# ScalarE in place of GpSimd multiplies the inputs of sequences 8 to 11 by their 1/rms in a diffusion block with attention

## Chip, cores and metric

One core of a Trainium2 chip runs the whole program in one launch. The metric is the device time of one execution in microseconds (us). The engines have separate instruction streams that run in program order and meet only at semaphores: TensorE (PE), VectorE (DVE), ScalarE (ACT), GpSimd (POOL) and SyncE (SP, which only issues transfers here).

## Reference

The input has 16 sequences of 128 tokens with 128 channels, all in float32. A transformer block with modulation by a condition (its first half is attention) is followed by a block of linear attention. What matters for the change is the beginning of the first block:

```python
def rmsnorm(x, w, eps=EPS):
    v = jnp.mean(x * x, axis=-1, keepdims=True)
    return w * (x * jax.lax.rsqrt(v + eps))

h = modulate(rmsnorm(x, norm1_w), sh_msa, sc_msa)   # x * (1 + scale) + shift, per sequence
qkv = (h @ qkv_w.T).reshape(B, N, 3, H, D)          # 16 heads of 8
q, k = rmsnorm(q), rmsnorm(k); q, k = rotated by the positions
attn = softmax(q @ k.T * D ** -0.5)
x = x + g_msa * ((attn @ v) @ proj_w.T + proj_b)
```

After that come a gated feed-forward network, and a second block with softmax over queries and keys, a context matrix per head, a layer norm and an output projection.

## The kernel before

One sequence (128 tokens on the partitions, 128 channels) is the unit of the attention part. After a prologue that brings sequences 0 to 5 through the projections, a loop of steps t = 0, 1, ... runs on four engines at once. It is written out by hand for each engine, and each engine works on another sequence of the pipeline in the same step. In step t, for the places that the change touches:

- **Input, sequence t+8.** `input_normed(b)` writes `xs` = x times `rstd_x`, a column with 1/rms of every token. `xs` has four buffers (NXS = 4). Sequences 0 to 3 are done by VectorE, 4 to 7 by ScalarE in the prologue, 8 to 15 by GpSimd in its steps 0 to 7 (L1114 to L1127).
- **1/rms of sequences 8 to 15.** GpSimd makes the column for all eight at once in its step 0, at the head of `input_normed(8)`: an affine operation on the mean squares (L1120) and a power of -1/2 (L1122), which raises the semaphore `p_rstd` to 3. The mean squares come from ScalarE before its step 0.
- **Projections, sequence t+6.** TensorE transposes `xs` (`input_turned(t + 6)`, L1962), ScalarE scales the result into `hT`, TensorE multiplies by the weights (L1969), and ScalarE copies q and k to `qk` and writes their squares to `sq`.
- **Heads, sequences t+5 and t+4.** VectorE sums the squares (`square_sums(t + 6)`, L1672) and for every odd sequence makes a first guess of 1/sqrt for two sequences at once (`seeds`, L1682 to L1687). GpSimd rotates q and k (`turned_partner(t + 5)`, `turned_own(t + 5)`, `added(t + 4)`), refines the guess in ten small operations in its even steps (`rsqrt_of_heads(t + 5)`, L1157 to L1175), and multiplies (`normed(t + 4)`, L1197, tile `qkpad`).
- **Keys and queries, sequence t+3.** TensorE transposes `qkpad` (`queries_and_keys(t + 3)`, L1940) once `normed` of that sequence is done; VectorE spreads the result over `kBD` (L1637) and `qTs` (L1645).
- **Scores, sequence t+2, and exponents, sequence t.** `round_(t, r)` on TensorE, r = 0 and 1, interleaves the scores of t+2 (L1890), whose row maxima VectorE takes (`rowmax`, L1608), with the scores again for the exponents of t (L1899), to which ScalarE applies Exp (`exp`, L1307, tile `probs`, four banks a step). Round r waits until both Exp of the round before have read their banks (`s_p`), and until VectorE has the maxima of the round before (`s_max`).
- **Values, sequence t.** TensorE multiplies `probs` by the values (L1995); ScalarE copies the result at the end of its step (`summed(t)`, L1376), spreads the values of t+6 (`values`, L1360) and sums squares of a finished sequence (`spread_of(t - 2)`, L1316).

So the order of work in a step is, on GpSimd: `turned_partner`, `rsqrt_of_heads`, `added`, `normed`, `input_normed`, `turned_own`, `input_biased`; on ScalarE: two Exp, `queries_and_max`, `modulated_input`, two Exp, `attended`, `squares`, `queries_keys`, `summed`, `values`, `spread_of`. The rest of the program (feed-forward in the last steps and behind the loop, then the second block) follows the loop on the same queues. The functions that the change touches, and the loops that call them:

Of the kernel before, what the change touches and what calls it, by code (L numbers as in the profile page):

```python
# [65 lines left out]
HEAD_B, MID_B, EARLY = 4, 8, 2  # L66
FIFTH6, FIVE4, THREE2 = -5.0 / 3.0, 1.25, 1.5
FRONT_B = 6
TBL = 4 * DH

LAST_A, LAST_POOL = B + 2, B + 1
# [5 lines left out]
def is_seq(b):  # L77

    return not isinstance(b, int) or 0 <= b < B


def wait(eng, sem, value):

    if not isinstance(value, int) or value > 0:
        eng.wait_ge(sem, value)
# [27 lines left out]
def dit_then_linear_attention(nc, x, cond, pos, norm1_w, qkv_w, q_norm_w, k_norm_w, proj_w, proj_b,  # L113
# [3 lines left out]
    with ctx:  # L117
        def sb(name, shape, dt=F32):
            return ctx.enter_context(nc.sbuf_tensor(name, shape, dt))

        def sem(name):
            return ctx.enter_context(nc.semaphore(name))
# [57 lines left out]
        turns = sb("turns", [128, B * AXES])  # L180
        rope = sb("rope", [128, B, TBL])

# [107 lines left out]
        p_rstd = sem("p_rstd")  # L290
# [12 lines left out]
        s_xs = sem("s_xs")  # L303
# [142 lines left out]
        def front_bank(b):  # L446

            return bank[O_BANK if b < FRONT_B and b % 2 else W_BANK]

# [606 lines left out]
        def _(g):  # L1056
# [57 lines left out]
            def input_normed(b):  # L1114

                if not is_seq(b):
                    return
                if b == MID_B:
                    g.wait_ge(pv_a, A_SQUARES)
                    q.tensor_scalar(ms[:, MID_B:], ms[:, MID_B:], 1.0, EPS0, ALU.mult, ALU.add).then_inc(p_ms, 1)  # L1120
                    g.wait_ge(p_ms, 1)
                    q.tensor_tensor(rstd_x[:, MID_B:], ms[:, MID_B:], minus_half[:, 0:B - MID_B], ALU.pow).then_inc(p_rstd, 1)  # L1122
                    g.wait_ge(p_rstd, 3)
                    g.wait_ge(s_xs, MID_B)
                wait(g, s_xsT, b - NXS + 1)
                q.tensor_tensor(xs[b % NXS][:, :], xin[:, b, :], rstd_x[:, b:b + 1].to_broadcast([128, D]),
                                ALU.mult).then_inc(s_xs, 1)  # L1127
# [128 lines left out]
        def _(a):  # L1256
# [44 lines left out]
            def exp(t, r, i):  # L1301

                if not is_seq(t):
                    return
                a.wait_ge((s_e0, s_e1)[i], ROUNDS * t + r + 1)
                wait(a, s_o, ROUNDS * (t - 1) + r + 1)
                q.activation(probs[2 * r + i][:, :, :, :].rearrange("p f a t -> p (f a t)"), exp_bank(t, r, i)[:, :],  # L1307
                             ACT.Exp, scale=SCALE).then_inc(s_p, 1)

            def spread_of(b):  # L1310

                if not is_seq(b):
                    return
                a.wait_ge(s_x1, b + 1)
                wait(a, s_sq1, b)
                q.activation(squared[:, :], x1[:, b, :], ACT.Square, scale=D ** -0.5, accum_out=ms1[:, b:b + 1]).then_inc(s_sq1, 1)  # L1316

            def modulated_input(b):

                if not is_seq(b):  # L1320
                    return
                a.wait_ge(s_xsT, b + 1)
                wait(a, s_qkv, b - 1)
                q.activation(hT[b % 2][:, :], front_bank(b)[:, 0:T], ACT.Identity, bias=mod(b, S1), scale=mod(b, A1)).then_inc(s_hT, 1)  # L1324

            def queries_and_max(b):

                if not is_seq(b):
                    return
                a.wait_ge(s_tp, b + 1)  # L1330
                wait(a, s_e0, ROUNDS * (b - 1))
                wait(a, s_e1, ROUNDS * (b - 1))
                q.activation(qTm[b % 2][:, :, :].rearrange("p f t -> p (f t)"), bank[P_BANK][:, 0:2 * T], ACT.Copy).then_inc(s_qTm, 1)

            def squares(b):

                if not is_seq(b):
                    return
                a.wait_ge(s_qkv, b + 1)
                wait(a, s_ss, b - 1)  # L1340
                q.activation(sq[b % 2][:, :, :].rearrange("p h d -> p (h d)"), front_bank(b)[:, 128:128 + 2 * D], ACT.Square).then_inc(s_sq, 1)

            def queries_keys(b):

                if not is_seq(b):
                    return
                wait(a, s_pa, b - NQK + 1)
                wait(a, s_r1, b - NQK + 1)
                q.activation(qk[b % NQK][:, :, :].rearrange("p h d -> p (h d)"), front_bank(b)[:, 128:128 + 2 * D], ACT.Copy).then_inc(s_qk, 1)  # L1349

            def values(b):

                if not is_seq(b):
                    return
                wait(a, s_o, ROUNDS * (b - NVP + 1))
                if b < NVP:
                    a.wait_ge(seeded_g, 2 * b + 2)
                spread = vpad[b % NVP][:, :].rearrange("p (a c) -> p a c", a=2)[:, :, 0:8 * VSTEP].rearrange(
                    "p a (i c) -> p i a c", c=VSTEP)[:, :, :, 0:DH]
                q.activation(spread, front_bank(b)[:, 384:512].rearrange("p (i a d) -> p i a d", i=8, a=2), ACT.Copy).then_inc(s_v, 1)  # L1360

            def attended(b):

                if not is_seq(b):
                    return
                a.wait_ge(s_oTp, b + 1)
                wait(a, s_proj, b)
                q.activation(oT[:, :], bank[P_BANK][:, 256:384], ACT.Copy).then_inc(s_oT, 1)

            def summed(b):  # L1370

                if not is_seq(b):
                    return
                a.wait_ge(s_o, ROUNDS * (b + 1))
                wait(a, s_oq, b)
                q.activation(oT4[:, :], bank[O_BANK][:, 0:2 * T], ACT.Copy).then_inc(s_oT4, 1)  # L1376
# [12 lines left out]

            def input_normed(b):  # L1390

                a.wait_ge(p_rstd, 2)
                a.wait_ge(s_xs, b)
                a.wait_ge(s_xsT, b - NXS + 1)
                q.activation(xs[b % NXS][:, :], xin[:, b, :], ACT.Identity, scale=rstd_x[:, b:b + 1]).then_inc(s_xs, 1)
# [29 lines left out]
            queries_keys(3)  # L1425
            values(3)
            input_normed(4)
            input_normed(5)
            modulated_input(4)
            weights(P_W1, bank[P_BANK][:, 0:FC * 128], w1T[:, :], 1.0)  # L1430
# [21 lines left out]
            for t in range(LAST_A):  # L1452
                exp(t, 0, 1)
                exp(t, 0, 0)
                if t == B - 1:
                    b_first(t - B)
                if t >= B:
                    b_first(t - B)
                if t >= B - 2:
                    b_input(t - B, t % 2)  # L1460
                queries_and_max(t + 1)
                modulated_input(t + 6)
                exp(t, 1, 0)
                exp(t, 1, 1)
                if t < B:
                    attended(t - 1)
                squares(t + 6)
                queries_keys(t + 6)
                if t >= B - 1:
                    b_rest(t - B)  # L1470
                if t >= B:
                    attended(t - 1)
                summed(t)
                values(t + 6)
                spread_of(t - 2)
                if t == B - 6:
                    a.wait_ge(ld_rest, N_REST)
                    q.activation(outw[:, :], outw_n[:, :], ACT.Copy, scale=0.5).then_inc(pv_a, 1)
                    q.activation(nbb[:, :], ident[:, :], ACT.Identity, bias=par[:, R_NB:R_NB + 1], scale=0.0).then_inc(pv_a, 1)
                    q.activation(lin[:, :, :].rearrange("p c f -> p (c f)"), lin_n[:, :, :].rearrange("p c f -> p (c f)"), ACT.Identity,  # L1480
                                 scale=par[:, R_NG:R_NG + 1]).then_inc(pv_a, 1)
# [293 lines left out]
        def _(e):  # L1775
# [53 lines left out]
            def modulation_rows():  # L1829

                e.wait_ge(pv_a, A_GB)
                e.wait_ge(s_v, FRONT_B)
                for k, src in enumerate((modr[:, 2, :], gbias[:, :], modr[:, 5, :])):
# [122 lines left out]
            def input_turned(b):  # L1956
# [3 lines left out]
                e.wait_ge(s_xs, b + 1)  # L1960
                wait(e, s_v, b - 1 if b < FRONT_B else b)
                q.transpose(front_bank(b)[:, 0:T], xs[b % NXS][:, :], ident[:, :]).then_inc(s_xsT, 1)  # L1962
# [16 lines left out]
            def weighted_values(b, r):  # L1979
# [4 lines left out]
                if r == 0:  # L1984
                    e.wait_ge(s_v, max(b + 1, FRONT_B))
                    wait(e, s_on, b)
# [118 lines left out]
```

## Time and profile before

| | |
|---|---|
| median of 3 runs | 206.25 us (206.19 to 206.61) |
| the profiled execution | 207.28 us, of which the span from its first to its last instruction is 205.6 us |
| mean granted TensorE clock | 0.992 of full speed |
| PE busy | 180.2 us (88% of the span) |
| DVE busy | 164.2 us (80%) |
| POOL busy | 141.0 us (69%) |
| ACT busy | 129.8 us (63%) |

Times in the trace count from the first instruction of the span. A share of busy time is a mean over stages with different limits, so the stage around steps 0 to 5 (about 29 to 65 us) has to be read by itself, from the timeline of each engine. In a timeline each row has the start, the length, the engine, the line and the operation; what stands in brackets at the end is how long the engine was idle before it and who ended that.

### The profile page before, as it was taken

The page shows a single profiled execution, that of the slowest core. Times are in us where ns is not written, and L with a number is a line of the kernel's source. Part 1 is how long each engine was busy: PE and PEld are TensorE (multiplying, and loading weights), DVE is VectorE, ACT ScalarE, POOL GpSimd, SP SyncE. Part 2 cuts the span into 40 slices and gives each one's busy share as a digit, 9 for nine tenths or more (in the row PEclk, how much of TensorE's full clock was granted, in tenths as well). Part 3 has the DMA queues.
Part 4 walks back from the last instruction along what each step waited for, and adds up shares of the span by engine and source line. Part 5 has one row for each costly group of instructions (what it writes and reads, how often), then busy time and mean ns, then how long its engine had stood idle before and what let it go on. Part 6 is the DMA issues. An engine that isn't in the chain of part 4 may idle for free.

```text
span 205.6 us, 6098 instructions
## 1 busy us (share of the span) xinstructions
PE 180.2 (88%) x2039; PEld 141.5 (69%) x2039; DVE 164.2 (80%) x495; ACT 129.8 (63%) x379; POOL 141.0 (69%) x333
## 2 busy tenths in 40 slices
PE   2598887997999999999999778899998899999954
PEld 2355565786687777787766557799997578887742
DVE  6799899896989999898765235678888789999871
ACT  1367798675867777767664764444443468999630
POOL 8889798998989897979700890445534847586651
PEclk9999999999999999999999999999999999999997
DMA  5955006800000000000000000000000000011111
GB/s 94 281 144 207 0 10 271 341 6 0 3 3 2 5 5 0 3 3 2 3 3 3 2 0 3 0 2 0 5 0 2 0 3 0 0 32 51 51 37 42
DMA packets 10428, 8.32 MB, mean 40 GB/s; under 512 B 3105, under 2 KB 9886, under 8 KB 9886
## 3 DMA queue, kind: packets, MB, share of 16 engines
q1 hardware_dynamic: 7006, 7.25, 10.2%
q10 hardware_dynamic: 3392, 0.68, 1.6%
q8 instruction: 17, 0.28, 0.5%
q14 instruction: 13, 0.11, 0.2%
HBM read 6.86 MB, written 1.07 MB: 39 GB/s over the span
## 4 chain that ended last, share of the span: by engine, by line
PE 45%; DVE 14%; issue 8%; ACT 6%; POOL 3%; POOLq 0%; ACTq 0%; DVEq 0%
PE bank L1890 5%; PE bank L880 5%; PE bank L868 5%; PE bank L869 4%; PE bank L1995 4%; DVE qkpad L1608 4%; PE bank L1899 4%; PE bank L997 2%; ACT probs L1307 2%; PE bank L913 2%; PE bank L1940 2%; PE bank L1927 2%; PE bank L1969 2%; PE bank L1915 1%; PE bank L977 1%
## 5 line engine op out<-in xcount | busy, mean ns | idle before, releaser
L1608 DVE TENSOR_REDUCE qkpad<-bank 128x4 f32<-128x512 f32 x64 | 41.0, 684 | 10.4 <-PE bank L1890 9.4
L1307 ACT ACTIVATE probs<-bank 128x512 f32<-128x512 f32 x64 | 34.7, 594 | 20.6 <-PE bank L1899 19.8
L1890 PE MATMUL bank<-kBD,qTs 32*128 32x256 f32 x224 | 32.0, 399 | 3.3 <-DVE qkpad L1608 2.2
L1899 PE MATMUL bank<-qTm,kBD 32*128 32x128 f32 x448 | 32.5, 283 | 0.0
L1899 PEld LDWEIGHTS bank<-qTm,kBD 32*128 32x128 f32 x448 | 27.1, 186 | 0.0
L1890 PEld LDWEIGHTS bank<-kBD,qTs 32*128 32x128 f32 x224 | 19.9, 184 | 9.4 <-DVE qkpad L1608 4.9
L579 ACT ACTIVATE th<-bank 128x256 f32<-128x256 f32 x24 | 9.2, 384 | 20.4 <-PE bank L869 17.0
L1995 PE MATMUL bank<-probs,vpad 128*32 128x128 f32 x512 | 18.5, 277 | 2.9 <-ACT probs L1307 2.9
L1995 PEld LDWEIGHTS bank<-probs,vpad 128*32 128x32 f32 x512 | 12.6, 109 | 9.3 <-ACT probs L1307 8.5
L1969 PE MATMUL bank<-qkvT,hT 128*128 128x384 f32 x32 | 15.4, 578 | 0.5 <-ACT hT L1324 0.5
L678 DVE SCALAR_TENSOR_TENSOR yg<-th,bank 128x256 f32<-128x256 f32 x24 | 10.1, 419 | 6.5 <-ACT th L579 6.5
L1940 PE MATMUL bank<-ident,qkpad 128*128 128x128 f32 x96 | 14.1, 277 | 1.1 <-POOL qkpad L1197 1.1
L1135 POOL TENSOR_TENSOR partner<-qk,rope 128x96 f32<-128x96 f32 x32 | 14.2, 466 | 0.8 <-ACT qk L1349 0.8
L509 POOL TENSOR_TENSOR x<-fg,x 128x256 f32<-128x256 f32 x6 | 4.4, 728 | 15.0 <-DVE fg L695 15.0
L868 PE MATMUL bank<-hT,w1T 128*128 128x256 f32 x48 | 14.4, 382 | 0.0
L869 PE MATMUL bank<-hT,w3T 128*128 128x256 f32 x48 | 14.3, 379 | 0.0
L880 PE MATMUL bank<-w2T,ff 128*128 128x128 f32 x96 | 13.2, 275 | 0.0
L519 POOL TENSOR_TENSOR rstd<-var,minus_half 128x2 f32<-128x2 f32 (+1 forms) x17 | 11.7, 691 | 1.4
L1940 PEld LDWEIGHTS bank<-ident,qkpad 128*128 128x128 f32 x96 | 10.8, 141 | 2.8 <-POOL qkpad L1197 1.7
L880 PEld LDWEIGHTS bank<-w2T,ff 128*128 128x128 f32 x96 | 12.4, 191 | 0.4
L1146 POOL TENSOR_TENSOR rot<-qk,rope 128x256 f32<-128x256 f32 x16 | 11.6, 728 | 0.0
L1197 POOL TENSOR_TENSOR qkpad<-rot,ny 128x256 f32<-128x256 f32 x15 | 9.7, 647 | 2.2 <-DVE ny L1705 0.4
(254 smaller groups left out, 527.6 us busy)
## 6 DMA issues: line engine op xcount, KB each, us to landing
gate<-in_cond_dram SPq DMA_DIRECT2D x1, 1024.0 KB, 4.7
x<-gate_rows SPq DMA_DIRECT2D x1, 1024.0 KB, 4.2
y<-gate_rows SPq DMA_DIRECT2D x1, 1024.0 KB, 6.3
res<-gate_rows SPq DMA_DIRECT2D x1, 1024.0 KB, 9.7
out_dram<-res SPq DMA_DIRECT2D x7, 128.0 KB, 1.8
xin<-in_x_dram ACTq DMA_DIRECT2D x2, 256.0 KB, 5.4
xin<-in_x_dram SPq DMA_DIRECT2D x1, 512.0 KB, 5.6
ada_n<-in_L_cond_ada_w_dram SPq DMA_DIRECT2D x1, 256.0 KB, 6.2
```

Of the source, the lines that this page charges most:

```text
L519: q.tensor_tensor(rstd[:, rows], var[:, rows], minus_half[:, 0:rows.stop - rows.start], ALU.pow).then_inc(made, 1)
L868: q.matmul(bank[GU_BANK[c]][:, 0:UNIT * T], w1T[:, c * 128:c * 128 + 128], flat(hT2[1 - p]), start=True, stop=True)
L869: q.matmul(bank[GU_BANK[c]][:, UNIT * T:], w3T[:, c * 128:c * 128 + 128], flat(hT2[1 - p]), start=True, stop=True).then_inc(b_gu, 1)
L880: last = q.matmul(bank[F_BANK[j]][:, 0:D], ff[c][:, j * T:(j + 1) * T], w2T[:, c, :], start=c == 0, stop=c == FC - 1)
L1135: last = q.tensor_tensor(heads(partner[b % 2][:, :, :])[:, :, :, k::2], heads(qk[b % NQK][:, :, :])[:, :, :, 1 - k:ROPE:2], table(b, 1)[:, ...
L1307: q.activation(probs[2 * r + i][:, :, :, :].rearrange("p f a t -> p (f a t)"), exp_bank(t, r, i)[:, :], ACT.Exp, scale=SCALE).then_inc(s_p, 1)
L1608: q.tensor_reduce(out_, score_bank(b, r, i)[:, :].rearrange("p (f a t) -> p f a t", f=2, a=2), X_AXIS, ALU.max, negate=True).then_inc(s_ma ...
L1890: last = q.matmul(bank[S_BANK[i]][:, f * 2 * T:(f + 1) * 2 * T], qTs[b % 2][rows, f, :], kBD[b % NKB][rows, f, :, :].rearrange("p a t -> p ...
L1899: last = q.matmul(bank[E_BANK[i]][:, (2 * f + k) * T:(2 * f + k + 1) * T], kBD[t % NKB][rows, f, k, :], qTm[t % 2][rows, f, :], start=True ...
L1940: last = q.transpose(dst[:, at_ + f * T:at_ + (f + 1) * T], qkpad[b % NKB][:, s, 8 * f:8 * f + 8, :].rearrange("p h d -> p (h d)"), ident[ ...
L1969: q.matmul(front_bank(b)[:, 128:512], hT[b % 2][:, :], qkvT[:, :], start=True, stop=True).then_inc(s_qkv, 1)
L1995: last = q.matmul(bank[O_BANK][32 * c:32 * c + 32, r * T:(r + 1) * T], vpad[b % NVP][:, col:col + VSTEP], probs[2 * r + i][:, f, k, :], st ...
```

## The change

ScalarE gets `input_normed(t + 8)` as the last piece of its steps 0 to 3. GpSimd still makes the column of 1/rms at the same place of its step 0, then returns, and resumes the multiplications with sequence 12 in its step 4.

```diff
+BY_ACT = 12
...
@@ GpSimd, input_normed(b)
                     q.tensor_tensor(rstd_x[:, MID_B:], ms[:, MID_B:], minus_half[:, 0:B - MID_B], ALU.pow).then_inc(p_rstd, 1)
+                if b < BY_ACT:
+                    return
+                if b == BY_ACT:
                     g.wait_ge(p_rstd, 3)
-                    g.wait_ge(s_xs, MID_B)
+                    g.wait_ge(s_xs, BY_ACT)
                 wait(g, s_xsT, b - NXS + 1)
@@ ScalarE, input_normed(b)
-                a.wait_ge(p_rstd, 2)
+                a.wait_ge(p_rstd, 2 if b < MID_B else 3)
                 a.wait_ge(s_xs, b)
                 a.wait_ge(s_xsT, b - NXS + 1)
                 q.activation(xs[b % NXS][:, :], xin[:, b, :], ACT.Identity, scale=rstd_x[:, b:b + 1]).then_inc(s_xs, 1)
@@ ScalarE, end of step t
                 spread_of(t - 2)
+                if MID_B <= t + 8 < BY_ACT:
+                    input_normed(t + 8)
```

The order on ScalarE at the end of its step 0, before the change (`qk2` and `vpad6` are of sequence 6, `oT4` closes sequence 0, `probs1` and `probs0` are the first two Exp of step 1):

```order
L1349 ACTIVATE qk2<-bank7 128x256 [waits s_r1,s_pa]
L1376 ACTIVATE oT4<-bank6 128x256 [waits s_o]
L1360 ACTIVATE vpad6<-bank7 128x8x2x8 [waits seeded_g]
L1307 ACTIVATE probs1<-bank3 128x512 [waits s_o,s_e1]
L1307 ACTIVATE probs0<-bank2 128x512 [waits s_o,s_e0]
L1333 ACTIVATE qTm0<-bank5 128x256 [waits s_e1,s_e0,s_tp]
```

and with it:

```order
L1353 ACTIVATE qk2<-bank7 128x256 [waits s_r1,s_pa]
L1380 ACTIVATE oT4<-bank6 128x256 [waits s_o]
L1364 ACTIVATE vpad6<-bank7 128x8x2x8 [waits seeded_g]
L1399 ACTIVATE xs0<-xin,rstd_x 128x128 [waits s_xsT,s_xs,p_rstd]
L1311 ACTIVATE probs1<-bank3 128x512 [waits s_o,s_e1]
L1311 ACTIVATE probs0<-bank2 128x512 [waits s_o,s_e0]
```

A multiplication (`xs0`, sequence 8) that waits for `p_rstd` now stands between the last copy of step 0 and the first Exp of step 1; the same stands at the ends of steps 1, 2 and 3.

The order on GpSimd at the end of its step 0, before (`qkpad0` is `normed(4)`, `rot1` is `turned_own(5)`, `partner0` belongs to sequence 6):

```order
L1197 TENSOR_TENSOR qkpad0<-rot0,ny0 128x32x8 [waits s_tp,s_ad,s_newton]
L1120 TENSOR_SCALAR ms<-ms 128x8 [waits pv_a]
L1122 TENSOR_TENSOR rstd_x<-ms,minus_half 128x8 [waits p_ms]
L1126 TENSOR_TENSOR xs0<-xin,rstd_x 128x128 [waits s_xsT,s_xs,p_rstd]
L1146 TENSOR_TENSOR rot1<-qk1,rope 128x256 [waits s_qk]
L1135 TENSOR_TENSOR partner0<-qk2,rope 128x96 [waits s_qk]
L1135 TENSOR_TENSOR partner0<-qk2,rope 128x96
```

and with the change:

```order
L1201 TENSOR_TENSOR qkpad0<-rot0,ny0 128x32x8 [waits s_tp,s_ad,s_newton]
L1121 TENSOR_SCALAR ms<-ms 128x8 [waits pv_a]
L1123 TENSOR_TENSOR rstd_x<-ms,minus_half 128x8 [waits p_ms]
L1150 TENSOR_TENSOR rot1<-qk1,rope 128x256 [waits s_qk]
L1139 TENSOR_TENSOR partner0<-qk2,rope 128x96 [waits s_qk]
L1139 TENSOR_TENSOR partner0<-qk2,rope 128x96
L1186 TENSOR_TENSOR rot1<-rot1,partner1 128x32x6 [waits s_r1]
```

The column `rstd_x` stays where it was, and `turned_own(5)` now follows it at once, without the multiplication in between. The order on TensorE, VectorE and SyncE is the same in both kernels.

## Rows read from the trace of the kernel before

**Rows 1.** The chain that ended last: start, length, work.

```profile
48.99 0.64 POOL qkpad L1197
49.67 0.66 PE bank L1940 x4
```

**Rows 2.** Timeline of POOL, steps 0 and 2.

```profile
37.20 1.66 POOL L1122 TENSOR_TENSOR rstd_x<-ms,minus_half 128x8 f32<-128x8 f32 x1
38.93 0.40 POOL L1126 TENSOR_TENSOR xs<-xin,rstd_x 128x128 f32<-128x128 f32 x1
39.29 0.73 POOL L1146 TENSOR_TENSOR rot<-qk,rope 128x256 f32<-128x256 f32 x1
...
44.45 0.29 POOL L1157 TENSOR_TENSOR nt<-ny 128x64 f32<-128x64 f32 x1
...
48.99 0.63 POOL L1197 TENSOR_TENSOR qkpad<-rot,ny 128x256 f32<-128x256 f32 x1
```

**Rows 3.** Timeline of ACT, end of the prologue to step 4.

```profile
27.04 0.87 ACT L1395 ACTIVATE xs<-xin,rstd_x 128x128 f32<-128x128 f32 x2
...
35.71 0.27 ACT L1360 ACTIVATE vpad<-bank 128x128 f32<-128x128 f32 x1
36.62 1.09 ACT L1307 ACTIVATE probs<-bank 128x512 f32<-128x512 f32 x2 [0.63 <-PE bank L1899]
...
47.87 1.08 ACT L1307 ACTIVATE probs<-bank 128x512 f32<-128x512 f32 x2 [0.35 <-PE bank L1899]
```

**Rows 4.** Timeline of PE, steps 1 to 4.

```profile
37.37 0.27 PE L1962 MATMUL bank<-ident,xs 128*128 128x128 f32 x1
37.85 0.48 PE L1890 MATMUL bank<-kBD,qTs 32*128 32x256 f32 x2 [0.20 <-DVE qkpad L1608]
...
42.56 0.82 PE L1940 MATMUL bank<-ident,qkpad 128*128 128x128 f32 x6
...
43.48 0.48 PE L1890 MATMUL bank<-kBD,qTs 32*128 32x256 f32 x2
...
48.19 0.38 PE L1940 MATMUL bank<-ident,qkpad 128*128 128x128 f32 x2
...
50.37 0.48 PE L1890 MATMUL bank<-kBD,qTs 32*128 32x256 f32 x2
...
56.45 0.48 PE L1890 MATMUL bank<-kBD,qTs 32*128 32x256 f32 x2 [0.44 <-DVE qkpad L1608]
```

**Rows 5.** Timeline of DVE, steps 1, 4 and 6.

```profile
41.73 0.50 DVE L1687 TENSOR_SCALAR ny<-nms 128x64 int32<-128x64 int32 x1
...
53.29 0.41 DVE L1672 TENSOR_REDUCE nms<-sq 128x32 f32<-128x256 f32 x1
...
55.12 1.28 DVE L1608 TENSOR_REDUCE qkpad<-bank 128x4 f32<-128x512 f32 x2
...
65.34 0.41 DVE L1672 TENSOR_REDUCE nms<-sq 128x32 f32<-128x256 f32 x1
...
66.77 1.28 DVE L1608 TENSOR_REDUCE qkpad<-bank 128x4 f32<-128x512 f32 x2
```

**Rows 6.** Two stretches: length, PE busy (instructions), granted clock, DMA share, GB/s.

```profile
48.57:49.67 1.10, 0.00 (x1) 1.00 0.00 0
199.00:204.00 5.00, 3.27 (x15) 0.66 0.13 39
```

**Rows 7.** Timeline of PE near the end.

```profile
196.65 0.33 PE L913 MATMUL bank<-ident,xs 128*128 128x128 f32 x1 [0.90 <-DVE xs L821]
196.82 0.60 PE L850 MATMUL bank<-warm 128*128 128x256 bf16 x4
197.26 0.41 PE L950 MATMUL bank<-outw,hs 128*128 128x128 f32 x2
...
199.46 0.39 PE L913 MATMUL bank<-ident,xs 128*128 128x128 f32 x1 [1.18 <-DVE xs L821]
199.65 1.06 PE L850 MATMUL bank<-warm 128*128 128x256 bf16 x4
200.51 0.63 PE L950 MATMUL bank<-outw,hs 128*128 128x128 f32 x2
```

## Prediction

> **What bounds the kernel now.** I read the chain that ended last first, then the timelines of GpSimd, ScalarE, TensorE and VectorE over steps 0 to 6, then the granted clock. The chain begins on GpSimd: `normed(6)` ends at 48.99 + 0.64 = 49.63 us, and TensorE takes up its transposes 0.04 us later [rows 1]. From there the chain runs without a break through TensorE and VectorE to the end. So GpSimd is late exactly once: in step 3 TensorE has done two of its six transposes at 48.19 and must wait with the other four. How much that costs is seen by the distance from the transposes to the second round of scores: 43.48 - 42.56 = 0.92 us in step 2, 50.37 - 48.19 = 2.18 us in step 3, a difference of **1.26 us** [rows 4]. In all other places of steps 1 to 6 TensorE waits little (0.20 and 0.44 us, both for row maxima of VectorE [rows 4]). The reader should see that ScalarE is not in this chain at that place, but that TensorE's second round waits for two Exp of ScalarE in every step.
>
> **What the change takes away.** Four multiplications of GpSimd, in its steps 0 to 3. One of them moves the next instruction by 39.29 - 38.93 = 0.36 us [rows 2]. Two of the four lie ahead of `normed(6)`, so GpSimd alone could be 0.72 us earlier there; that is the whole gain, and it would come out of the 1.26 us. The other two lie behind it, where GpSimd has ceased to be late, and I cost them at nothing.
>
> **What it adds, step 0.** The column of 1/rms is made by GpSimd from 37.20 to 37.20 + 1.66 = 38.86 [rows 2], at the end of a queue that the change does not shorten: nothing is removed ahead of it. ScalarE has finished its step 0 at 35.71 + 0.27 = 35.98 and starts the Exp pair of step 1 at 36.62 [rows 3]. With the change the multiplication of sequence 8 stands between these two and needs the column. It can begin at 38.86 + 0.07 = 38.93 (0.07 is the handover that GpSimd's own multiplication shows [rows 2]), and takes 0.43, half of a pair of the same instruction in the prologue, 0.87 [rows 3]. So the Exp pair starts at 39.36 instead of 36.62, **2.74 us late**. Queued behind it on ScalarE are the Exp pair, `qTm`, `hT` of sequence 7, the second Exp pair, and the squares and copies of sequence 7. No table has to be loaded for it: the same function runs between the Exp already, as `hT`.
>
> TensorE has nothing to hide that. Its last transpose of step 1 ends at 37.37 + 0.27 = 37.64, and the second round started at 37.85 [rows 4]. Now it needs the Exp pair, which ends at 39.36 + 1.09 = 40.45; with a handover of 0.04 that is 40.49, **2.64 us later** than before, and TensorE stands still from 37.64 to 40.49, for 2.85 us. VectorE, which waits for the scores of that round, moves with it.
>
> **Steps 1 to 3.** Their multiplications have their column. They cost ScalarE 0.43 each, in gaps such as the 0.35 us ahead of the Exp pair at 47.87 [rows 3]. The excess of 0.08 stays hidden: that pair ends at 47.87 + 1.08 = 48.95, and TensorE would want it at 50.37 - 1.26 = 49.11 at the earliest [rows 3, 4]. Without this cover it would be 0.08 us a step.
>
> **What comes back in step 3.** The delay of 2.64 us makes TensorE reach the transposes at 48.19 + 2.64 = 50.83 [rows 4]. GpSimd is not free to use its lead: its refinement for sequence 7 waits for VectorE's guess, which ended at 41.73 + 0.50 = 42.23 [rows 5] and now ends at 44.87. With the handover it starts at 44.94 instead of 44.45 [rows 2], 0.49 late, and `normed(6)` ends at 49.62 + 0.49 = 50.11 [rows 2]. That is still ahead of TensorE, so the whole 1.26 us vanishes, though by TensorE's lateness and not by GpSimd's lead. Left: 2.64 - 1.26 = 1.38.
>
> **What comes back in step 4.** There the second round waited 0.44 us for VectorE [rows 4]. The same VectorE work, from the sum of squares to the maxima, took 55.12 - 53.29 = 1.83 us in step 4 and 66.77 - 65.34 = 1.43 us in step 6 [rows 5]. With GpSimd now waiting for VectorE, as it does in step 6, step 4 should look like step 6; I take 0.3 of these 0.40 us, between nothing and the whole 0.44. The delay is then **1.1 us** (0.94 to 1.38). Behind step 4 every engine is shifted alike, the chain is unbroken, and no transfer with a fixed time is left to meet, so I let it go through to the end.
>
> **The clock of TensorE.** A gap of 2.85 us between matmuls occurs nowhere in this part of the trace. At a gap of 1.10 us the granted clock stayed at full speed, 2.4 GHz [rows 6]. Near the end it fell: TensorE was idle for 0.90 us, worked, and was idle for 1.18 us [rows 7]; in the 5 us from 199 the mean clock was 0.66, which is (1 - 0.66) x 5 / 0.5 = 3.4 us at half speed, 1.2 GHz [rows 6]. The idle time before that fall, 2.08 us in two pieces, is less than the 2.85 us that the change makes in one. So I expect a fall here too, of about that length. Its price comes from the warm-up matmuls at either level: four of them advance in 197.26 - 196.82 = 0.44 us at full speed and in 200.51 - 199.65 = 0.86 us at half [rows 7]. A fully busy TensorE then loses 1 - 0.44/0.86 = 0.49 of the stretch, 1.66 us of 3.4; some 0.7 us of it should fall into the gap itself, which leaves 2.7 x 0.49 = **1.3 us**. Bounds: nothing (no fall), and 1.66.
>
> A rule speaks against this term. The Trainium skill (TensorE: Matmul & The Clock Gate, section Why this matters for your kernels) advises only to keep gaps between bursts of matmuls under a limit, and a single gap of this size would pass it; by that advice the sum would end without the clock term, as in the first rival. The fall behind the two shorter gaps [rows 7] does not agree with reading the advice as a guarantee.
>
> **Sum.** 1.1 + 1.3 = 2.4 us. The working was done inside one execution of 207.28 us (span 205.6), 1.03 above the median of the runs; as it consists of differences only, I add it to the median: 206.25 + 2.4 = 208.65, given as **208.6 us**.
>
> **Rivals.**
> 1. *The wait is paid, the clock holds.* 206.25 + 1.1 = 207.35 us, between 207.2 and 207.6. For it: the full clock through the gap of 1.10 us [rows 6]; against it: the fall near the end. Chance 0.27.
> 2. *The clock is low for two such stretches,* because the first is followed by a TensorE that still waits for VectorE. 208.65 + 1.3 = 209.95 us. For it: TensorE was still meeting waits of 0.44 us in step 4 [rows 4]; against it: at half speed TensorE is the slow engine and hardly idle. Chance 0.07.
> 3. *Faster: ScalarE does not wait in step 0, and GpSimd's lead counts.* The place is the column of 1/rms: if it were written before 36.62 - 0.43 - 0.07 = 36.12, the multiplication would vanish in ScalarE's gap, and `normed(6)` would come 0.72 us earlier: 206.25 - 0.72 = 205.53 us. It is written at 38.86 [rows 2], 2.7 us past that point; only GpSimd's spans in the profile being far too long would save it. Chance 0.04.
> 4. *The delay is made up on the way,* because work behind step 4 has slack that the chain does not show: 206.25 us or a little more. The unbroken chain speaks against it. Chance 0.04.
>
> That the change does not do what it says is excluded by the order: ScalarE's stream has the four instructions more and GpSimd's four fewer.
>
> **How the numbers follow.** The forecast has 0.58; its own range is 206.25 + 0.94 + 1.0 = 208.2 to 206.25 + 1.38 + 1.66 = 209.3. With the first rival, 0.85 of the chance lies between 207.2 and 209.3, which I widen by 0.1 each way for the spread of the runs: 207.1 to 209.4. A measurement of this kernel tells about 0.2% (0.4 us) from no change. Faster by more than that is rival 3, 0.04; within it is rival 4, 0.04; slower are the forecast and rivals 1 and 2, 0.92.
>
> **What would show it.** Right: ScalarE idle for nearly 3 us ahead of the multiplication of sequence 8, released by the line that makes the column; TensorE idle for about 2.85 us ahead of the second round of step 1; no wait for `qkpad` in step 3; GpSimd waiting for VectorE's guess already at sequence 7. The clock term is right if the granted clock shows some 3.4 us at half speed at about 39 to 46 us. Wrong: an Exp pair of step 1 that starts before 38 us; a TensorE that still waits for `normed(6)`; or a distance to the old kernel that shrinks behind step 5, which would mean slack that I did not see.

## The result, and the profile after

The changed kernel takes **208.62 us** (median of 4 runs, 208.28 to 209.56) against 206.38 us (206.19 to 206.61): a ratio of 1.0113, with a 95% interval of 1.0087 to 1.0138. It is slower by about 1.1%, as forecast; the forecast time was 208.6 us, in a range of 207.1 to 209.4. The ratios in this document are of each kernel's fast executions and are no quotients of the two medians, from which they differ by up to 0.3%.

The profiled execution took 208.37 us with a span of 206.6. One thing has to be known before the two profiles are compared. In the one before, TensorE's clock was low for 3.4 us near the end [rows 6]; in the one after it was not, as the stretch from 199 to 206 us shows (columns as in rows 6):

```profile
199.00:206.00 7.00, 3.39 (x28) 1.00 0.19 56
```

The two spans differ by 1.0 us, but the kernels differ by more. The place to compare them is the loop, ahead of that stretch. The start of the second round of scores in each step, from the timelines of TensorE (us):

| step | 1 | 2 | 3 | 4 | 6 | 8 |
|---|---|---|---|---|---|---|
| before | 37.85 | 43.48 | 50.37 | 56.45 | 68.11 | 79.46 |
| after | 40.42 | 47.66 | 53.28 | 58.90 | 70.18 | 81.53 |
| later by | 2.57 | 4.18 | 2.91 | 2.45 | 2.07 | 2.07 |

The change loses 2.57 us in step 1, another 1.61 by step 2, and gets back 1.27 in step 3, 0.46 in step 4 and 0.38 by step 6. What stays is **2.07 us**, and it stays to the end: the same operation of VectorE starts at 198.58 us before (`xs`, L821) and at 200.65 after. The two lowest times of the kernel before are 206.19 and 206.25 us; 206.2 + 2.07 = 208.3 is about the two lowest of the change, 208.28 and 208.37.

**Step 0 and 1.** The timeline of ScalarE answers to [rows 3]:

```profile
35.74 0.27 ACT L1364 ACTIVATE vpad<-bank 128x128 f32<-128x128 f32 x1
38.91 0.40 ACT L1399 ACTIVATE xs<-xin,rstd_x 128x128 f32<-128x128 f32 x1 [2.90 <-POOL rstd_x L1123]
39.22 1.06 ACT L1311 ACTIVATE probs<-bank 128x512 f32<-128x512 f32 x2
...
51.60 0.40 ACT L1399 ACTIVATE xs<-xin,rstd_x 128x128 f32<-128x128 f32 x1
52.05 1.09 ACT L1311 ACTIVATE probs<-bank 128x512 f32<-128x512 f32 x2
```

ScalarE stands still for 2.90 us behind its last copy, released by the line that makes the column, and the Exp pair starts at 39.22 instead of 36.62. At the end of step 2 the same multiplication (51.60) needs no wait. The chain that ended last now runs through that column, some 12 us ahead of the `normed(6)` of [rows 1]:

```profile
37.22 1.67 POOL rstd_x L1123
...
39.69 0.60 ACT probs L1311
40.42 0.45 PE bank L1896
```

TensorE, to be set against [rows 4]:

```profile
37.40 0.27 PE L1968 MATMUL bank<-ident,xs 128*128 128x128 f32 x1
40.42 0.65 PE L1896 MATMUL bank<-kBD,qTs 32*128 32x256 f32 x2 [2.75 <-ACT probs L1311]
...
45.11 0.48 PE L1896 MATMUL bank<-kBD,qTs 32*128 32x256 f32 x2
...
47.66 0.48 PE L1896 MATMUL bank<-kBD,qTs 32*128 32x256 f32 x2
...
52.38 0.82 PE L1946 MATMUL bank<-ident,qkpad 128*128 128x128 f32 x6
...
53.28 0.48 PE L1896 MATMUL bank<-kBD,qTs 32*128 32x256 f32 x2
...
58.90 0.48 PE L1896 MATMUL bank<-kBD,qTs 32*128 32x256 f32 x2
```

The gap ahead of the second round of step 1 is 2.75 us, released by ScalarE's Exp. In step 3 all six transposes go in one piece (52.38), with no wait for `qkpad`; in step 4 there is no wait for row maxima (58.90). The granted clock in the stretches around the gap (columns as in rows 6):

```profile
37.40:40.42 3.02, 0.27 (x3) 1.00 0.96 399
40.42:40.70 0.28, 0.28 (x6) 0.85 0.08 29
40.70:44.00 3.30, 3.30 (x27) 0.50 0.02 7
44.00:45.00 1.00, 1.00 (x33) 0.99 0.00 0
```

It is at full speed, 2.4 GHz, through the gap, and falls to half, 1.2 GHz, just behind it, for about 3.4 us. In that time the first matmuls of the round take 0.65 us where they took 0.48, and TensorE arrives at step 2 another 1.61 us late.

**GpSimd**, to be set against [rows 2]:

```profile
37.22 1.65 POOL L1123 TENSOR_TENSOR rstd_x<-ms,minus_half 128x8 f32<-128x8 f32 x1
38.84 0.73 POOL L1150 TENSOR_TENSOR rot<-qk,rope 128x256 f32<-128x256 f32 x1
...
45.11 0.89 POOL L1139 TENSOR_TENSOR partner<-qk,rope 128x96 f32<-128x96 f32 x2 [2.32 <-ACT qk L1353]
46.36 0.29 POOL L1161 TENSOR_TENSOR nt<-ny 128x64 f32<-128x64 f32 x1 [0.36 <-DVE ny L1693]
...
50.76 0.63 POOL L1201 TENSOR_TENSOR qkpad<-rot,ny 128x256 f32<-128x256 f32 x1
...
55.28 0.46 POOL L1233 TENSOR_TENSOR xin<-xin,y 128x128 f32<-128x128 f32 x1
56.42 0.89 POOL L1139 TENSOR_TENSOR partner<-qk,rope 128x96 f32<-128x96 f32 x2 [0.68 <-ACT qk L1353]
```

`turned_own(5)` follows the column at 38.84, 0.45 us earlier than before. But the lead is lost: GpSimd waits 2.32 us for `qk` of sequence 7 from the late ScalarE, then for VectorE's guess, and `normed(6)` starts at 50.76 instead of 48.99.

### The profile page after: what moved, and what is told of

Read it like the earlier page. It is cut to its first block, busy times and chain, and to the rows that moved or that the text cites. A ratio compares the mean times of both kernels' runs of the same rounds, so it can differ in the third digit from the quotient of the medians.

```text
span 206.6 us, 6102 instructions
## 1 busy us (share of the span) xinstructions
PE 179.5 (87%) x2039; PEld 141.1 (68%) x2039; DVE 163.5 (79%) x495; ACT 131.0 (63%) x383; POOL 139.3 (67%) x329
## 4 chain that ended last, share of the span: by engine, by line
PE 56%; DVE 9%; issue 7%; ACT 6%; POOL 4%; POOLq 0%; ACTq 0%; DVEq 0%
PE bank L1896 8%; PE bank L2001 6%; PE bank L1905 5%; PE bank L881 5%; PE bank L869 5%; PE bank L870 4%; PE bank L1975 4%; PE bank L1946 3%; PE bank L1933 3%; ACT probs L1311 2%; PE bank L998 2%; PE bank L914 2%; DVE qkpad L1614 2%; PE bank L1941 1%; PE bank L1921 1%
## 5 line engine op out<-in xcount | busy, mean ns | idle before, releaser
L1896 PE MATMUL bank<-kBD,qTs 32*128 32x256 f32 x224 | 32.8, 406 | 5.0 <-ACT probs L1311 2.8
L1905 PE MATMUL bank<-qTm,kBD 32*128 32x128 f32 x448 | 33.3, 288 | 0.0
L1896 PEld LDWEIGHTS bank<-kBD,qTs 32*128 32x128 f32 x224 | 20.6, 187 | 11.0 <-issue 6.1
L1905 PEld LDWEIGHTS bank<-qTm,kBD 32*128 32x128 f32 x448 | 27.8, 190 | 0.0
L1975 PE MATMUL bank<-qkvT,hT 128*128 128x384 f32 x32 | 16.0, 596 | 0.5 <-ACT hT L1328 0.5
```

What stands on the lines that cost most here:

```text
L1896: last = q.matmul(bank[S_BANK[i]][:, f * 2 * T:(f + 1) * 2 * T], qTs[b % 2][rows, f, :], kBD[b % NKB][rows, f, :, :].rearrange("p a t -> p ...
L1905: last = q.matmul(bank[E_BANK[i]][:, (2 * f + k) * T:(2 * f + k + 1) * T], kBD[t % NKB][rows, f, k, :], qTm[t % 2][rows, f, :], start=True ...
L1975: q.matmul(front_bank(b)[:, 128:512], hT[b % 2][:, :], qkvT[:, :], start=True, stop=True).then_inc(s_qkv, 1)
```

## Experiments

The theory: ScalarE's wait for the column makes TensorE late (2.6 us, mostly made up by step 6) and makes its clock fall (1.6 us, not made up). The rivals: ScalarE's added work is the loss; or the low clock costs nothing; or the loss is in proportion to the wait. The first four kernels ran on one chip, beside a kernel before of 206.18 us (21 runs); the next four on another, beside 206.31 us (14 runs); four further profiles on a third, beside 205.97 us (one run).

**GpSimd keeps sequence 8.** ScalarE's multiplications stay at the ends of steps 1 to 3 only.

```diff
@@ GpSimd, input_normed(b)
-                if b < BY_ACT:
+                if MID_B < b < BY_ACT:
                     return
-                if b == BY_ACT:
+                if b in (MID_B, BY_ACT):
                     g.wait_ge(p_rstd, 3)
-                    g.wait_ge(s_xs, BY_ACT)
+                    g.wait_ge(s_xs, b)
@@ ScalarE
-                if MID_B <= t + 8 < BY_ACT:
+                if MID_B < t + 8 < BY_ACT:
```

> GpSimd multiplies sequence 8 again, right behind the column of 1/rms; ScalarE keeps 9, 10 and 11 at the ends of its steps 1 to 3. Theory (the loss is ScalarE's wait for the column in step 0): the wait is gone, TensorE's gap in step 1 is 0.2 us as before, the clock holds there, and of GpSimd's saving one multiplication of 0.36 us lies ahead of normed(6): 206.25 - 0.36 = 205.9 us (205.7 to 206.3). Rival (the loss is ScalarE's added work of 0.4 us a step): three of the four multiplications are still there, so about three quarters of the loss of some 2.1 us: 207.8 us.

Measured: 205.30 us (205.29 to 205.61), ratio 0.9969 (0.9957 to 0.9981). The rival of added work falls: with three of the four multiplications the kernel is faster than before. It is also faster than expected. TensorE's waits in the timeline, and the wait of step 6 in the kernel before, which stands in no group of rows:

```profile
37.92 0.48 PE L1896 MATMUL bank<-kBD,qTs 32*128 32x256 f32 x2 [0.23 <-DVE qkpad L1614]
...
49.34 0.66 PE L1946 MATMUL bank<-ident,qkpad 128*128 128x128 f32 x4 [0.71 <-POOL qkpad L1201]
...
55.84 0.48 PE L1896 MATMUL bank<-kBD,qTs 32*128 32x256 f32 x2 [0.16 <-DVE qkpad L1614]
```

```profile
68.11 0.48 PE L1890 MATMUL bank<-kBD,qTs 32*128 32x256 f32 x2 [0.40 <-DVE qkpad L1608]
```

The gap in step 1 is as before. The wait for `normed(6)` shrank from 1.10 [rows 6] to 0.71 us, by 0.39 where 0.36 was expected; yet the kernel gained more, because the wait for row maxima in step 4 shrank too, from 0.44 [rows 4] to 0.16, and that of step 6, 0.40 before, is gone (second rounds at 50.04, 55.84, 67.17 and 78.49 in steps 3, 4, 6 and 8: 0.33, 0.61, 0.94 and 0.97 us earlier than before).

**The change with TensorE kept busy in the gap.**

```diff
                 queries_and_keys(t + 3)
+                if t == 1:
+                    e.wait_ge(warmed, 1)
+                    e.wait_ge(s_v, 7)
+                    for _ in range(23):
+                        q.matmul(front_bank(7)[:, 0:256], warm[:, 0:128], warm[:, 0:256], start=True, stop=True)
                 input_turned(t + 6)
```

> The change, with 23 warm-up matmuls of TensorE (the kind that it uses near the end, 0.11 us each, 2.5 us together) ahead of its last transpose of step 1, where it stands still otherwise; their result is overwritten. Theory (wait and clock are two separate terms): ScalarE still waits 2.9 us, the second round of step 1 still starts 2.6 us late, but the granted clock stays at full speed, and the 1.61 us that TensorE lost between that round and the next are not lost: 206.25 + 2.57 - 1.27 (the wait for normed(6)) - 0.4 to 0.9 (VectorE's waits) = 206.7 to 207.2 us. Rival (the low clock costs nothing, because the other engines set the pace there): the same as the change, 208.3 us.

Measured: 207.0 us (206.7 to 207.9), ratio 1.0061 (1.0044 to 1.0079). The timeline of TensorE, and two stretches of its clock (columns as in rows 6):

```profile
40.39 0.48 PE L1896 MATMUL bank<-kBD,qTs 32*128 32x256 f32 x2 [0.25 <-ACT probs L1311]
...
46.01 0.48 PE L1896 MATMUL bank<-kBD,qTs 32*128 32x256 f32 x2
```

```profile
37.40:40.40 3.00, 2.75 (x27) 1.00 0.66 273
40.40:44.00 3.60, 3.60 (x72) 1.00 0.01 5
```

The second round of step 1 is as late as in the change, 40.39 against 40.42, and still released by ScalarE, but the clock holds, and step 2 starts its second round at 46.01 instead of 47.66: 1.65 us earlier. By step 8 (79.89) this kernel is only 0.43 us behind the one before, where the change is 2.07 behind. So of the 2.07 us **1.64 are the clock's and 0.43 the wait's**. The difference of 0.42 us is still there near the end (`xs`, L822, at 199.00 against 198.58). The rival that the low clock costs nothing falls.

**The wait alone.** The kernel before, ScalarE waits for the column and does nothing with it.

```diff
                 spread_of(t - 2)
+                if t == 0:
+                    a.wait_ge(p_rstd, 3)
```

> The kernel before, with one edit: ScalarE waits at the end of its step 0 for the column of 1/rms, and does nothing with it; GpSimd multiplies all of 8 to 15 as before. Theory: the Exp pair of step 1 comes 38.93 - 36.62 = 2.3 us late, TensorE idles about 2.5 us, and the loss is the change's less 0.3 to 0.4: 207.9 us (207.6 to 208.3) if the clock falls in that gap, 206.6 if it holds. Rival (ScalarE's added work, or the missing work of GpSimd, is what matters): 206.25 us.

Measured: 207.41 us (206.51 to 209.09), ratio 1.0067 (1.0039 to 1.0094). A wait without any work moved makes the kernel slower, so neither the added nor the removed work is needed for the loss. The times do not lie around their middle: four of ten executions took 206.5 to 206.7 us, five 207.8 to 209.1. Two more executions were profiled to see why.

> A second profiled execution of the kernel before with ScalarE's wait alone (gap of 2.46 us). The first, of 206.68 us, kept full speed. An execution above 207.7 us should show half speed behind the gap in step 1, and the second round of step 2 some 1.6 us later than in the first (45.81 us); if it shows half speed only near the end, the gap of 2.46 us is too short for a fall.

> A third profiled execution of the same, for the same question.

They took 209.16 and 207.90 us. TensorE in the first profile (206.68 us), and in the second (209.16 us):

```profile
40.17 0.48 PE L1892 MATMUL bank<-kBD,qTs 32*128 32x256 f32 x2 [2.46 <-ACT probs L1307]
...
45.81 0.48 PE L1892 MATMUL bank<-kBD,qTs 32*128 32x256 f32 x2
```

```profile
40.13 0.48 PE L1892 MATMUL bank<-kBD,qTs 32*128 32x256 f32 x2 [2.47 <-ACT probs L1307]
...
47.32 0.48 PE L1892 MATMUL bank<-kBD,qTs 32*128 32x256 f32 x2
```

The gaps are equal, 2.46 and 2.47 us, and the round behind them starts at the same time. In the first the mean clock of the whole execution was 1.00. In the second the clock was at half speed behind the gap, and at full speed again from 44 us on (two of its stretches):

```profile
41.00:42.00 1.00, 1.00 (x16) 0.50 0.00 0
...
44.00:45.00 1.00, 1.00 (x38) 1.00 0.00 0
```

The next round starts at 47.32 instead of 45.81, 1.51 us later. In the third it is 47.26. So the same gap in the same kernel lets the clock fall in some executions and not in others, and this is most of the difference between their times. (The execution of 209.16 us was also low for 3.4 us near its end.) The ten timed executions agree: the four of 206.5 to 206.7 us had a mean clock of 1.00, the five of 207.8 us and more one of 0.984 to 0.992. What decides between the two is not shown.

**ScalarE's work alone.** The kernel before, with four more multiplications into a tile that nobody reads.

```diff
+        spare = sb("spare", [128, D])
...
                 spread_of(t - 2)
+                if t < 4:
+                    q.activation(spare[:, :], xin[:, t + 8, :], ACT.Identity, scale=rstd_x[:, t:t + 1])
```

> The kernel before, with one edit: ScalarE does four more multiplications of the same size at the ends of its steps 0 to 3, with a column that has long been there, into a tile that nobody reads; GpSimd multiplies as before. Theory: 0.43 us each lie in ScalarE's gaps of 0.35 to 0.64 us: 206.25 us (206.2 to 206.5). Rival (ScalarE's added work is the loss): about 208.3 us.

Measured: 206.11 us (205.89 to 207.53), ratio 1.0004 (0.9984 to 1.0024). The work costs nothing that can be measured.

**The change one step later.**

```diff
-                if MID_B <= t + 8 < BY_ACT:
-                    input_normed(t + 8)
+                if MID_B <= t + 7 < BY_ACT:
+                    input_normed(t + 7)
```

> The change, one step later: ScalarE multiplies sequences 8 to 11 at the ends of its steps 1 to 4 (TensorE needs sequence 8 in its step 2), GpSimd goes on with 12 in its step 4. Theory: the column is two microseconds old when ScalarE wants it, so no wait in step 1 and no fall of the clock; GpSimd is 0.72 us earlier at normed(6), twice what leaving it sequence 8 gave (that kernel was 0.8 to 0.9 us faster than the one before): 204.9 us (204.7 to 205.3). Rival (ScalarE's added work costs, or GpSimd's lead is worth nothing beyond the first 0.36 us): 205.3 to 205.5 us. Against the theory: GpSimd has to wait in its step 4 until ScalarE has written sequence 11.

Measured: 205.19 us (205.07 to 205.71), ratio 0.9950 (0.9938 to 0.9961). The time lies inside the expected bounds, but hardly below that of the kernel in which GpSimd keeps sequence 8 (205.30, on the other chip), so the rival that GpSimd's lead is worth little beyond its first 0.36 us is not excluded by this run. GpSimd and TensorE:

```profile
60.28 0.40 POOL L1130 TENSOR_TENSOR xs<-xin,rstd_x 128x128 f32<-128x128 f32 x1 [0.61 <-issue]
```

```profile
44.42 0.48 PE L1896 MATMUL bank<-kBD,qTs 32*128 32x256 f32 x2 [0.58 <-DVE qkpad L1614]
```

GpSimd stands still for 0.61 us in step 4 ahead of sequence 12. The profile names no releaser, but ScalarE's multiplication of sequence 11, which it has to wait for, ends only at 59.75 + 0.40 = 60.15; that was feared. TensorE meets a wait of 0.58 us for row maxima in step 2 that was not expected.

**The same for all of sequences 8 to 15.** The version one step later, with one constant changed.

```diff
-BY_ACT = 12
+BY_ACT = 16
```

> As the version one step later, but ScalarE multiplies all of sequences 8 to 15, at the ends of its steps 1 to 8, and GpSimd none. Theory: as that version or up to 0.3 us faster, since GpSimd need not wait for ScalarE in step 4 and touches VectorE less: 204.7 us (204.4 to 205.2). Rival (ScalarE's added work costs): 0.08 us a step more, 205.3 us or above.

Measured: **204.72 us** (204.70 to 204.81), ratio 0.9920 (0.9907 to 0.9933): faster than both kernels of the study. TensorE's only waits between 34 and 80 us:

```profile
37.79 0.48 PE L1896 MATMUL bank<-kBD,qTs 32*128 32x256 f32 x2 [0.22 <-DVE qkpad L1614]
...
44.02 0.48 PE L1896 MATMUL bank<-kBD,qTs 32*128 32x256 f32 x2 [0.59 <-DVE qkpad L1614]
```

The waits for `normed(6)` and for the row maxima of steps 4 and 6 are all gone; the new one of step 2 remains. Eight multiplications on ScalarE cost nothing that shows.

**Half the column first.** The change, with two powers of four columns in place of one of eight.

```diff
-                    q.tensor_tensor(rstd_x[:, MID_B:], ms[:, MID_B:], minus_half[:, 0:B - MID_B], ALU.pow).then_inc(p_rstd, 1)
+                    q.tensor_tensor(rstd_x[:, MID_B:BY_ACT], ms[:, MID_B:BY_ACT], minus_half[:, 0:BY_ACT - MID_B], ALU.pow).then_inc(p_rstd, 1)
+                    q.tensor_tensor(rstd_x[:, BY_ACT:], ms[:, BY_ACT:], minus_half[:, 0:B - BY_ACT], ALU.pow).then_inc(p_rstd, 1)
...
-                    g.wait_ge(p_rstd, 3)
+                    g.wait_ge(p_rstd, 4)
```

> The change, but GpSimd makes the column for sequences 8 to 11 first and for 12 to 15 right behind it. A power of four columns took 1.03 us in the prologue, one of eight 1.66, so ScalarE's wait ends 0.63 us earlier and TensorE's gap in step 1 is 2.1 us instead of 2.75. Theory (a long gap lets the clock fall, the wait by itself is nearly made up by step 8): the clock holds in most executions and the time is 206.3 us (206.2 to 206.8). Rival (the loss is proportional to the wait): 0.63 of 2.74 us less of the loss of 2.1 us: 207.8 us.

Measured: 207.17 us (206.07 to 207.81), ratio 1.0028 (1.0004 to 1.0052). The gap is 2.12 us as worked out. Four of nine executions took 206.07 to 206.15 us, about the theory's value; that the others would be few was wrong, and the median lies outside the theory's range. The profiled one (207.17 us) was low near the end and not in step 1, so two more were profiled.

> A second profiled execution of the half column (gap of 2.1 us in step 1). Its times fell into two groups, 206.1 and 207.2 to 207.8 us, and the first profile, of 207.17 us, shows full speed in the gap and a low stretch near the end. If the slower group is executions in which the clock fell in step 1, one of about 207.7 us shows half speed behind the gap there; if it is always the stretch near the end, none does. An execution of 206.1 us shows neither.

> A third profiled execution of the same, for the same question.

They took 206.15 and 209.20 us. TensorE's gap in the one and in the other, and stretches of the clock in the second:

```profile
39.86 0.48 PE L1897 MATMUL bank<-kBD,qTs 32*128 32x256 f32 x2 [2.13 <-ACT probs L1312]
```

```profile
39.92 0.80 PE L1897 MATMUL bank<-kBD,qTs 32*128 32x256 f32 x2 [2.13 <-ACT probs L1312]
```

```profile
40.00:41.00 1.00, 1.00 (x16) 0.50 0.04 16
...
45.00:46.00 1.00, 1.00 (x21) 0.50 0.00 0
46.00:47.00 1.00, 1.00 (x24) 0.78 0.00 0
```

With the same gap of 2.13 us the clock held in the first execution, and in the second it was low for twice as long as in the change, about 6.8 us. The rival in proportion to the wait falls with the first: 2.1 us of waiting cost nothing there, for its second round of step 8 starts at 79.41 us, where the kernel before starts it at 79.46.

**The change once more.**

> The change once more, beside the others on one chip, for the spread of its executions. Theory: 208.3 us where the clock falls once, in step 1; 206.7 to 207.0 us in an execution where it holds; about 1.1 us more where it also falls near the end, as it does in some executions of every kernel here. Rival (the 208.6 us of the first runs were a chance of their chip): under 207.5 us as a median.

Measured: 209.03 us (206.63 to 209.89), ratio 1.0102 (1.0059 to 1.0145). One of the six executions took 206.63 us, at a mean clock of 1.00: the change in an execution in which the clock did not fall. The profiled one (208.58 us) shows the fall behind the gap, and none near the end.

## Why the prediction was right

**The place and the wait: right.** Forecast: the multiplication at 38.93, the Exp pair at 39.36, TensorE's second round at 40.49 behind a gap of 2.85 us. Measured: 38.91, 39.22, 40.42 and 2.75. The multiplication holds ScalarE for 0.31 us rather than 0.43, because the Exp starts before it has ended.

**Steps 1 to 3 at nothing: right,** shown by ScalarE's work alone and by the version in which it does all eight.

**What comes back in step 3: right,** 1.27 us for 1.26, by TensorE's lateness and not by GpSimd's lead. `normed(6)` was later than worked out (it ended at 51.39 and not 50.11), since the low clock also delayed the `qk` and the guess that GpSimd waits for: with TensorE kept busy in the gap it ended at 49.18 + 0.63 = 49.81. TensorE, at 52.38, was later still.

**What comes back in step 4: mis-sized.** I took 0.3 us of VectorE's wait and let the rest go through to the end. Step 4 gave 0.46, the whole wait of 0.44, and step 6 another 0.38. So the sentence that behind step 4 every engine is shifted alike was wrong, and the sign that was named for it came: the delay shrank behind step 5, from 2.46 us there to 2.07 in step 6. The prediction names waits of 0.20 and 0.44 us as all that TensorE meets besides in steps 1 to 6; it overlooked the 0.40 us of step 6 (68.11 us, shown above), and took this step as the standard for step 4. The kernel with TensorE kept busy in the gap shows the wait without the clock: 2.54 us in step 1, 51.63 - 50.37 = 1.26 behind step 3 (forecast 1.38), 57.25 - 56.45 = 0.80 behind step 4 (forecast 1.1, at least 0.94), 68.53 - 68.11 = 0.42 behind step 6.

Where VectorE's time came from is seen in three of its rows after:

```profile
55.79 0.28 DVE L1671 TENSOR_TENSOR x<-x1g,xin 128x128 f32<-128x128 f32 x1
56.10 0.42 DVE L1678 TENSOR_REDUCE nms<-sq 128x32 f32<-128x256 f32 x1
...
57.51 1.29 DVE L1614 TENSOR_REDUCE qkpad<-bank 128x4 f32<-128x512 f32 x2
```

and in the first row's counterpart before, with the row of GpSimd beside it:

```profile
52.74 0.62 DVE L1665 TENSOR_TENSOR x<-x1g,xin 128x128 f32<-128x128 f32 x1
```

```profile
52.58 0.63 POOL L1197 TENSOR_TENSOR qkpad<-rot,ny 128x256 f32<-128x256 f32 x1
```

The addition takes 0.28 us after and 0.62 before, in the same step. Before, GpSimd worked beside it (`normed(7)`, until 53.21); after, GpSimd had finished at 55.28 + 0.46 = 55.74 and waited until 56.42. From the sum of squares to the maxima it is 57.51 - 56.10 = 1.41 us, where it was 1.83 [rows 5]. The Trainium skill (SBUF — State Buffer, section SBUF: two separate sides) says that a VectorE operation with two inputs in SBUF and a GpSimd operation that reads SBUF exclude each other for a whole instruction. The two lengths of the addition agree with it. The 0.42 us between the sum of squares and the maxima lies in operations with one input tile, of which that sentence does not speak. What causes the VectorE time that came back was not isolated by a run.

**The clock: right that it falls, mis-sized at 1.3 us.** It is 1.61 to 1.65 us, nearly the upper bound of 1.66. The deduction of 0.7 us for a part of the low stretch that would fall into the gap was the error: in the profile the fall came some 0.2 us behind the end of the gap, and all of the stretch met a busy TensorE. (The lower 1.0 us of the forecast's own range has no working in the prediction.) In the execution of the half column that took 209.20 us it began inside the gap and lasted twice as long, so one deduction for all executions does not exist.

**The two sizes erred in opposite directions.** The wait is worth 0.43 us and not 1.1, the clock 1.64 and not 1.3; together 2.07 for 2.4. The trace alone would have given 208.3 us. The median is higher because in two of the four executions the mean clock was lower still (0.982 and 0.989, against 0.992 in the two fastest). Where it was low in them no profile shows: near the end, as in the profile before, or longer in step 1, as in the half column. The agreement of 208.6 with 208.62 is luck to that extent; the six executions of the second set had a median of 209.03.

**The rivals.** The first (the clock holds) happened in one of the ten timed executions of the change, at 206.63 us, not at 207.35: its price had the wrong size of the wait in it. The second (twice as long a low clock) was seen in an execution of the half column, at 209.20 us, but not for the reason given: TensorE was busy all the time from 40 to 46 us. Whether the executions of the change at 209.5 to 209.9 us (mean clock 0.982 to 0.984) were such cases is not known. The third (faster) did not happen, but its mechanism is real: with GpSimd's lead free to count, the same move one step later is faster than the kernel before by 0.5%. Its gain was sized too small: 0.72 us for the four sequences, which gave 206.31 - 205.19 = 1.1. The fourth (the delay is made up on the way) is true of most of the wait, 2.54 us of which 0.43 were left, and of all of it in the half column at full clock; the clock's loss was not made up.

## What to carry to other kernels

When a piece of work moves to an idle engine, ask not only how long it takes there but when its inputs are ready: on an engine that runs in order, a wait holds up everything behind it, and here the same move one step later turned a loss of 1.1% into a gain of 0.5%. A stall of TensorE can cost more through its clock than through its length: of the 2.07 us that a gap of 2.75 us cost here, 1.64 were the clock's. Where the stall can't be removed, dummy matmuls can fill it; here they got 1.6 of 2.1 us back. Delays that pass through a pipeline with waits in it are partly absorbed by those waits, and each of the waits has to be looked at, not only the first two.

## What the runs showed that was not expected

- The clock fell at the end of, or just behind, gaps of 2.75, 2.47 and 2.13 us between matmuls in some executions, and held behind gaps of 2.46 and 2.13 us in other executions of the same kernels. What decides it is open. The Trainium skill (TensorE: Matmul & The Clock Gate, section Why this matters for your kernels) advises to keep such gaps under a limit that all of these keep; by that rule none should have cost the clock, and the runs do not agree.
- A fall lasted 3.4 us in most profiles and about 6.8 us in one.
- With the clock at full speed, a delay of 2.5 us in step 1 left 0.43 us in step 8.
